# Addresses of a chunk's eight windows formed in one row ahead of each loop

## The reference

```python
h = relu(layernorm(x))
neigh = segment_sum(h[src], dst)                      # layer 0 (GIN)
x = x + relu(relu(((1 + eps) * h + neigh) @ W1 + b1) @ W2 + b2)
h = relu(layernorm(x)); hn = layernorm(h) * gamma + beta   # layer 1 (attention)
t = gelu(concat(hn[src], edge_attr) @ Wt + bt)
attn = sum((t @ Wk + bk) * (hn[dst] @ Wq + bq)) * edge_weight / sqrt(128)
m = segment_max(attn, dst); e = exp(attn - m[dst])
a = e / (segment_sum(e, dst)[dst] + 1e-16)
x = x + h + gelu(segment_sum(a * (t @ Wv + bv), dst))      # h is this layer's residual
```

## Time and profile before

| | |
|---|---|
| median of three timed runs | 4087.96 us |
| span of the profiled execution | 6013.6 us |
| total time of the profiled execution around its span | not shown |
| PE busy | 3985.3 us (66%) |
| POOL busy | 3043.9 us (51%) |
| DVE busy | 1961.7 us (33%) |
| ACT busy | 1601.6 us (27%) |
| granted TensorE clock, mean | 0.633 of full speed |
| GIN stage in the profile | to about 2460 us |

### The profile page before, as it was taken

The page is one execution under the profiler, slowest core; times in us unless marked ns, Lnnn a source line. Parts: engine busy times, 40 slices in busy tenths (PEclk is TensorE's granted clock), DMA queues, the critical chain, the costliest instruction groups (busy, mean ns, idle before and its releaser), DMA issues.

```text
span 6013.6 us, 75137 instructions
## 1 busy us (share of the span) xinstructions
PE 3985.3 (66%) x19120; PEld 3071.2 (51%) x19121; DVE 1961.7 (33%) x6898; ACT 1601.6 (27%) x3223; POOL 3043.9 (51%) x3332
## 2 busy tenths in 40 slices
PE   1466666555555555577777777777777777777777
PEld 1344444444434444355555555556555565555655
DVE  4222222222222222233333333333333333333344
ACT  4222222222222222322222222222222222222223
POOL 4566666666666666344444444444444444444442
PEclk5555555555565555577766667766676666766677
DMA  4122222222222222222222222222222222222222
GB/s 128 53 68 66 65 67 66 65 67 67 66 65 68 66 65 67 62 81 77 81 77 77 82 76 80 78 78 81 75 81 77 76 82 76 81 77 77 82 77 65
DMA packets 390065, 446.29 MB, mean 74 GB/s; under 512 B 111768, under 2 KB 314734, under 8 KB 390000
## 3 DMA queue, kind: packets, MB, share of 16 engines
q1 hardware_dynamic: 276940, 233.83, 13.3%
q0 software_dynamic: 100096, 205.20, 13.1%
q10 hardware_dynamic: 12964, 6.53, 0.4%
HBM read 387.05 MB, written 58.21 MB: 74 GB/s over the span
## 4 chain that ended last, share of the span: by engine, by line
another core or an unknown queue 28%; PE 25%; ACT 3%; issue 2%; DVE 0%; DVEq 0%; ACTq 0%
PE attention_sum_ps L1210 10%; PE attention_t_ps L1153 4%; PE attention_pre_ps L1144 3%; PE attention_sc_q L1167 3%; PE attention_row_bank L1189 2%; PE attention_pre_ps L1140 2%; ACT attention_tT L1281 2%; ACT attention_t L1285 1%; PE attention_tot_ps L1219 1%; PE attention_tot_ps L1202 1%; PE attention_sum_ps L1201 0%; DVE attention_lines L1419 0%; ACT acc L1043 0%; PE attention_xm_bank L1175 0%
## 5 line engine op out<-in xcount | busy, mean ns | idle before, releaser
L514 POOL DMA_INDIRECT attention_t<-source_rows,attention_idx x1548 | 1471.4, 951 | 496.0 <-issue 496.0
L514 POOL DMA_INDIRECT gin_hs<-h_rows,gin_idx x1500 | 1455.8, 971 | 486.1 <-issue 486.1
L508 POOL TENSOR_TENSOR spare<-ones 1x1 f32<-1x1 f32 x195 | 36.0, 184 | 1892.9 <-PE attention_sum_ps L1210 1376.9
L1281 ACT ACTIVATE attention_tT<-attention_pre_ps 128x512 f32<-128x512 f32 x391 | 233.5, 597 | 1883.5 <-remote 1381.9
L1167 PE MATMUL attention_sc_q<-attention_qw,attention_tT 128*128 x3128 | 590.7, 329 | 187.7 <-issue 187.6
L1167 PEld LDWEIGHTS attention_sc_q<-attention_qw,attention_tT 128*128 128x128 f32 x3128 | 540.7, 247 | 215.6 <-issue 215.4
L698 PE MATMUL gin_sums<-gin_hot,gin_hs 128*128 128x40 f32 x3136 | 612.2, 383 | 0.0
L1210 PE MATMUL attention_sum_ps<-attention_e_hot,attention_t 128*128 128x96 f32 x3072 | 607.5, 389 | 0.0
L698 PEld LDWEIGHTS gin_sums<-gin_hot,gin_hs 128*128 128x128 f32 x3136 | 598.1, 297 | 18.2 <-issue 12.6
L1210 PEld LDWEIGHTS attention_sum_ps<-attention_e_hot,attention_t 128*128 128x128 f32 x3072 | 591.8, 301 | 21.4 <-issue 20.9
L706 PE MATMUL gin_uy_bank<-acc,gin_w_W 128*128 x196 | 118.6, 708 | 727.2 <-DVE acc L926 727.1
(11 more groups left out here) (215 smaller groups left out, 5319.1 us busy)
## 6 DMA issues: line engine op xcount, KB each, us to landing
attention_evT<-in_edge_attr_cols SPq DMA_DIRECT2D x196, 512.0 KB
attention_t<-source_rows,attention_idx POOLq DMA_INDIRECT x1548
gin_hs<-h_rows,gin_idx POOLq DMA_INDIRECT x1500
attention_qw<-qk_cols SPq DMA_DIRECT2D x98, 160.0 KB, 3.2
attention_cw<-qk_bias_cols SPq DMA_DIRECT2D x98, 132.0 KB, 3.9
attention_fade<-fades SPq DMA_DIRECT2D x98, 132.0 KB, 3.8
gin_x<-in_x SPq DMA_DIRECT2D x98, 128.0 KB
residual_rows<-gin_r SPq DMA_DIRECT2D x98, 128.0 KB
```

Of the source, the lines that this page charges most:

```text
L514: gp.indirect_dma_start(out=out[:, k, :], out_offset=None, in_=rows[:, :], compute_op=op, in_offset=bass.IndirectOffsetOnAxis(ap=idx[:, k: ...
L1281: act.activation(tT[q % 2][:, :], pre_ps[:, :], ACT.Gelu).then_inc(s["tT_sb"], 1)
```

## The change

Ahead of each loop over a chunk's blocks, the eight starts are read, the addresses of the eight views are formed in one row, and a no-operation that names them keeps them there. The loops then use the ready addresses. This is done on PE in `add_rows` (GIN), `scores` (once per chunk, for all four quads), `sums` and `totals`, and on DVE in `score`, `raise_maxima` and `below_maxima`. In `raise_maxima` the eight values of `raised` to wait for are also formed ahead. The operations, their order and their semaphores stay.

```diff
+def addresses(eng, views):
+
+    eng.keepalive_nop([eng.lower_ap(view) for view in views])
...
                         pe.matmul(sums[j][:, 0:SPAN], zeros[0:1, 0:P], zeros[:, :], start=True, stop=True, skip_group_check=True)
-                        for b in range(BPC):
-                            off = inside(pe, pe_regs[b])
+                        offs = [inside(pe, reg) for reg in pe_regs]
+                        addresses(pe, [sums[j][:, bass.ds(off, WIN)] for off in offs])
+                        for b, off in enumerate(offs):
...
-                    def scores(f, q):
+                    def score_windows(f):
+                        offs = [inside(pe, reg) for reg in pe_regs[f.k]]
+                        addresses(pe, [qw[f.j][:, bass.ds(off, WIDE)] for off in offs])
+                        return offs
+
+                    def scores(f, q, offs):
...
                         for n in range(4 * q, 4 * q + 4):
-                            if n % SUB == 0:
-                                off = inside(pe, pe_regs[f.k][n // SUB])
...
-                                           qw[j][:, bass.ds(off, WIDE)], start=True, stop=True)
+                                           qw[j][:, bass.ds(offs[n // SUB], WIDE)], start=True, stop=True)
...
                     def sums(bk, blocks=range(BPC)):
                         j = bk.j
-                        for b in blocks:
-                            off = inside(pe, pe_regs[bk.k][b])
+                        offs = {b: inside(pe, pe_regs[bk.k][b]) for b in blocks}
+                        addresses(pe, [sum_of(bk)[:, bass.ds(off, WIDE)] for off in offs.values()])
+                        for b, off in offs.items():
...
                     def totals(bk):
+                        offs = [inside(pe, reg) for reg in pe_regs[bk.k]]
                         wait(pe, s["pairs"], bk.c + 1)
-                        for b, reg in enumerate(pe_regs[bk.k]):
-                            off = inside(pe, reg)
+                        addresses(pe, [tot_of(bk)[0:33, bass.ds(off, WIN)] for off in offs])
+                        for b, off in enumerate(offs):
...
                             turn_gelu(f, 0)
-                            scores(f, 0)
+                            offs = score_windows(f)
+                            scores(f, 0, offs)
...
                     def score(f):
                         c, h, j = f.c, f.h, f.j
                         load_offsets(v, block_regs, g, c)
-                        for b in range(BPC):
-                            off = inside(v, block_regs[b])
+                        offs = [inside(v, reg) for reg in block_regs]
+                        addresses(v, [cw[j][:, bass.ds(off, WIN)] for off in offs])
+                        for b, off in enumerate(offs):
...
+                    def raised_at(c, b):
+                        at = BPC * c + b
+                        return at if isinstance(at, int) else v.to_reg(at)
...
                         offs = [inside(v, reg) for reg in block_regs]
+                        addresses(v, [mnew[0:1, bass.ds(off, WIN)] for off in offs])
+                        turns = [raised_at(c, b) for b in range(BPC)]
                         for b, off in enumerate(offs):
                             some = mnew[0:1, bass.ds(off, WIN)]
...
-                            wait(v, s["raised"], BPC * c + b)
+                            wait(v, s["raised"], turns[b])
...
                     def below_maxima(bk, offs):
 
                         c, h, j = bk.c, bk.h, bk.j
+                        addresses(v, [row_bank[:, bass.ds(off, WIN)] for off in offs])
                         for b, off in enumerate(offs):
```

More of the change, by code:

```diff
@@ L1256, in step @@
                             turn_gelu(f, 1)
-                            scores(f, 1)
+                            scores(f, 1, offs)
                         if mid:
@@ L1265, in step @@
                             turn_gelu(f, 2)
-                            scores(f, 2)
+                            scores(f, 2, offs)
                             if not f.last:
                                 turn_gelu(f, 3)
-                                scores(f, 3)
+                                scores(f, 3, offs)
                         if mid:
```

## The result

The changed kernel takes 4094.72 us (median of 12 runs, 4087.57 to 4104.63), the kernel before, on the same chip, 4089.31 us (12 runs, 4084.49 to 4094.4). The ratio, which is taken over all the runs and not of the two medians (5.4 us apart), is 1.0018, with a 95% interval of 1.0011 to 1.0026: some 7 us slower, where 3 us faster was forecast.

A forecast was written before the change was run, and what follows sets the result against it. POOL's gathers were taken to bound both stages, their terms summing to 4202 us, 114 us over the median. From the median of 4088 us, 3 us gained at the end gave 4085 us; the range was 4035 to 4100 us.

The forecast's parts named there:

- GIN's row lies under its 7 us: 0: PE's row in GIN's sums: free, as GIN's step of 12.9 us leaves 7 us to spare under its gathers.
- P's account: A theory of the experiments, not the forecast: the open row makes PE's step the one that sets the pace.
- The rival that ended slower: PE's row lies open in attention's totals, 0.3 us a chunk: 29 us slower, 4117 us; chance 0.14.
- The bound: POOL's gathers, one every 1.25 us, set the pace in both stages; a chunk of 16 costs 20.4 us.
- the likeliest case: Whole kernel: gathers bind and the end gains 3 us, giving 4080 to 4090 us; chance 0.46.
- The lag: What PE has finished reaches other engines some 8 to 13 us late in the first profile; taken as the recording's.
- the 114 us that my sum had too much: Gathers and uncovered stretches summed to 4202 us, 114 us over the median; put down to 36 ns a gather.
- the rival in which the attention step binds: Attention's step of 19.0 to 19.9 us sets the pace: 4039 us once the gathers catch the gain; chance 0.29.
- DVE's gain: Attention's running maxima and other DVE steps: 0.8 to 1.1 us a chunk sooner, ending in waits while gathers bind.
- The 3 us at the end: The last two or three attention steps, which no gather covers, gain up to 0.9 us each, some 3 us.
- The range made of it for PE: PE's rows ahead of the matmuls: 0 to 0.3 us a chunk later by the queue rule; 0 was taken.
- L: A theory of the experiments, not the forecast: a DVE instruction with both operands in SBUF holds up gathers starting under it.

The follow-up runs named there:

- dve_only: Kernel before with only DVE's rows of the change and none of PE's: 4082.64 us, ratio 0.9997 to the kernel before.
- att_all: Changed kernel with GIN's `add_rows` left as in the kernel before: 4079.07 us, ratio 0.9996 to the kernel before.
- att_all_ps2: Changed kernel with GIN's `add_rows` as before, and the one-hot's column numbers and the residual's y in PSUM: 4074.18 us, ratio 0.9965.
- after_ps2: Changed kernel with the one-hot's column numbers and the residual's y moved to PSUM: 4084.05 us, ratio 0.9985 to the kernel before.
- before_again: The kernel before, unchanged, run and recorded again: 4084.09 us, ratio 1.0000.
- gin_early: Kernel before with only GIN's row, put with its register load ahead of the waits in `add_rows`: 4093.93 us, ratio 1.0021.
- late_b: Kernel before with an extra DVE reduction of 800 columns ahead of GIN's one-hot: 4127.31 us, ratio 1.0106.
- late_b_ps: `late_b` with the one-hot's column numbers copied to PSUM: 4082.24 us, ratio 1.0002 to the kernel before.
- before_ps: Kernel before with the one-hot's column numbers copied to PSUM: 4076.26 us, ratio 0.9985.

## Why the prediction was wrong

- **The step that failed** is "GIN's row lies under its 7 us: 0". The slack is real: PE idles about 3 us ahead of each chunk's sums in both kernels, and by P's account the row costs nothing. But a later result was treated as free because no one waits for it. What follows it on DVE, the one-hot and the residual's two additions, is no one's bottleneck either; it moves against the gathers, which are, and holds some of them up. By the profile that is 7.3 us at GIN's last gather in place of the 0. What DVE's addition, and all that follows it in DVE's order, shares with POOL's gathers isn't asked in the forecast.
- **The rival that ended slower** had the right row and the wrong place and price. It put an open row of 0.3 us into attention's totals, at 29 us. In GIN's sums the row opens 0.35 us (0.3 was worked out, as "in the totals and in GIN's sums the wait stands ahead of the row"), and 0.35 x 98 = 34 us would be its price if it set the pace; through the gathers it costs a fifth.
- **The bound was right**, and is now shown on a recording without lag: gathers 1.25 us apart in both stages, with a median duration of 944 or 945 ns before and after. That the time, 4094.72 us, lies within the range is luck: the likeliest case was to be 4080 to 4090 us, and the range reached to 4100 only for the row in attention's totals, which had no part in it.
- **The lag was the recording's**, as taken: it is in no other one. But the 114 us that my sum had too much were not in the gathers, as I put it (36 ns each): their pitch is 1.249 us in the clean recording. A change of chunk is 1.30 us there and not 1.61 (196 x 0.31 = 61 us), from GIN's last gather to attention's first are 29.6 us and not 71, behind the last gather 52.6 and not 69: 119 us together. Two more terms nearly cancel: the wait for the normalised rows is 29.6 us and not 64.0, and the distances within a chunk average 1.260 us and not 1.25, over 2932 of them 30 us more. A chunk of attention is so 20.2 us, not 19.8, and its step at 19.0 to 19.9 lies under it: the rival in which the attention step binds had less for it than its 0.29.
- **DVE's gain: right, and so is that it ends in a wait.** L1419's eight take 1.72 us (1.6 to 1.8 forecast), and the 0.67 us a chunk are back in DVE's wait for the broadcast, 3.48 us for 2.82. The way there was another than the forecast's: PE didn't wait for the maxima, so nothing came sooner behind them. `dve_only` is at 0.9997.
- **The 3 us at the end** can't be told from nothing: `att_all`, which holds all of attention's rows, is at 0.9996, its interval reaching to 1.0005.
- **The queue of 64 instructions** that the Trainium skill gives TensorE (Advanced Engine Details and Errata, Engine Queue Depths) led the forecast to expect that steps between products are hidden and a row ahead of them may not be. The trace agrees: 0.30 us became 0.65. The range made of it for PE, 0 to 0.3 us a chunk, was about right for the sums and said nothing of what the sums then move.
- **What stays open.** That the addition and the one-hot lie further apart in the fourth chunk of a turn I put down to the loop's branch on DVE, which stands there; that wasn't tested. The row's 8 us between `att_all_ps2` and `after_ps2` are explained by L in part and untested. And the attention stage has 66 to 95 gaps over 1.3 us. In `before_again` 77 of its 82 have one of five instructions of DVE over the gather's start that have both operands in SBUF (L1389, L1390, L1411, L1422, L1424), and no gather so covered is short; whether moving an operand to PSUM would take them away wasn't tried.

## What to carry to other kernels

Where one engine's stream sets the pace and another shares something with it, an edit on a third engine is not free because it is hidden: ask which instructions it shifts, and by how much against that stream. Plot the pace-setter's gaps against the start of the suspected instruction; a gap that grows one for one with the overlap is a lock. Take the sharing away, here by one operand moved from SBUF to PSUM, rather than tune the moment, for `gin_early` shows that moving it can miss in either direction. Then look again: here the next instruction with two operands in SBUF took the place of those that were freed.

## What the runs showed of the hardware

- A gather issued by POOL, 0.94 us long, waits for an instruction of DVE with two SBUF operands that starts 0.04 us or more ahead of it and ends more than 0.13 us behind its recorded start, until that instruction ends: for the one-hot of 0.82 us up to 0.54 us more on a gap of 1.25 in the table's means (1.787 us), and up to 1.90 in single gaps. The same instruction with one operand in PSUM costs it nothing (1.248 us, 74 gathers).
- Where DVE runs straight into such an instruction from another, a gather that starts under the first waits for the second as well: 13 gathers of `late_b`, the longest gap 2.77 us. With one operand of the second in PSUM (`late_b_ps`) none of 19 did.
- POOL's operation of 0.18 us on SBUF (`hold`) takes 0.42 us in the row of `after_ps2` in which DVE's L929, with two SBUF operands, started 0.05 us ahead of it.
- The wait can fall on DVE instead: the 11 one-hots of `before_again` that start less than 0.05 us ahead of a gather take 0.87 us on average, those of `before_ps`, with one operand in PSUM, 0.82.
- DVE's addition to the nodes, which has one operand in PSUM, runs from 1170.43 to 1170.86 in the rows of `before_again`, over the start of the gather of 1170.69 and the moment behind it, and leaves it at 0.94 us. In attention the same one-hot line (L440) reads its column numbers from PSUM, and the 55 gathers of `before_again` that start under it are 1.250 us from the next.
- Eight register steps of 44 ns between products cost PE nothing; packed into one of 173 and three of 74 ns ahead of them, they put off the first product by 0.35 us.
